# A four-stage decoder kernel: 32-wide heads moved to quarters of the array, score blocks issued in pairs, and the last stage's tail put in the order of one batch after the other

## The chip, the cores and the metric

The kernel runs on one core of a Trainium2 chip. The time is the device time of one execution in microseconds. Before the change it was 4651.4 us, the median of three runs (4647.05 to 4660.06).

## The reference

The input `x` is four batches of 512 tokens by 256 channels. It passes six sublayers, each with a residual and a layer norm. All matrix products are in 32-bit floats unless the text says otherwise.

```
x = LN(x + L0_attn(x))          # 16 heads of 64, with a zero key
x = LN(x + L0_xattn(x, ctx))    # 16 heads of 16, masked; softmax(q k^T / 4, -1e9 where mask == 0) v
x = LN(x + L0_ffn(x))           # top-2 of 8 experts
x = LN(x + L1_attn(x))          # 4 state-space layers with a scan over the 512 tokens
x = LN(x + L1_xattn(x, ctx))    # see below
x = LN(x + L1_ffn(x))           # gate, up and down with rounded activations and ternary weights

L1_xattn: x1 = LN(x + (x Wv) Wsa)                       # the self attention sees only its own token
          x2 = LN(x1 + MHA(x1, ctx) Wmha)               # 8 heads of 32, 512 keys
          y  = LN(x2 + relu(x2 W1) W2)
```

## The kernel before

Five engines run programs written out by hand and meet by counting semaphores: TensorE (`pe`, PE in the profile), VectorE (`v`, DVE), ScalarE (`act`, ACT), GpSimd (`pool`, POOL) and the queue of loads and stores (`sp`, SP). On each engine the instructions stand in program order. A wait holds back everything behind it on its engine. PSUM has eight banks of 512 words, `PS[:, 0..7, :]`.

The stages follow one another: for each of the four batches attention A (`AT_A`, 16 heads of 64) and attention B (`AT_B`, the masked one, its heads of 16 padded to 32), then the experts, then the state-space layers, then the last stage (`AT_E`, 8 heads of 32, and the feed-forward part), which takes the batches in two rounds `r` of a pair `p = 0, 1`.

**An attention** is `attend`, written once for each engine. A step `i` is two heads by 128 query tokens. B has 32 steps, E 16 for each batch. In the steady state a step goes through these hands:

- PE multiplies queries by keys into two of four score banks (L1147).
- DVE takes the row maxima. In B it adds the mask on the way and writes the sum to `b_S` in SBUF (L1589, then L1592 for the sign). In E one instruction does it (L1597).
- ACT takes the exponentials and their sums (L806).
- DVE inverts the sums (L1615), and POOL scales the probabilities (L641).
- PE transposes the probabilities of the step three before (L1159) into banks 4 and 5. DVE copies bank 4 (L1604) and ACT copies bank 5 (L816) to `pT`.
- PE multiplies the values by the transposed probabilities, one of four key blocks for each step (L1176), into bank 6 or 7.

In one turn of its loop PE does scores of step `i`, transposes of step `i - 3`, values of step `i - 7`. The next transposes wait for both copies of the last ones (`pt_a`, `pt_v`), since they go to the same banks.

A step of four-heads-to-128-rows attention (`per == 4`: B and E) takes two heads that lie in different halves of the array's rows. The queries are stored twice, each copy with every second strip of 32 rows zeroed, so that a product over 64 rows yields one head. ACT makes both copies (`pj_q`, L788). The value product writes 32 PSUM rows for each of the two heads, 512 columns each.

**The last stage** runs every phase for batch 0 of the pair and then for batch 1: context and its keys and values, layer norm 3, value and output projection, layer norm 4, queries, both attentions, output projection, layer norm 5, first and second linear layer of both batches, layer norms 6 and 7 of both, rounding of both, the loop of the feed-forward part over eight tiles (the batches alternate), layer norm 8 of both, and the stores. `sum_up` adds the residual to each tile and then, in one instruction, the bias (L1930). `ln_a` is the statistics and `ln_b` the rest of a layer norm.

Of the kernel before, what the change touches and what calls it, by code (L numbers as in the profile page):

```python
# [43 lines left out]
Q_WIDE = 2  # L44
# [9 lines left out]
class Count:  # L54
# [3 lines left out]
    def __init__(self, n, p, starts=None, batches=4):  # L58
        self.n, self.p, self.first = n, p, batches * p
        self.starts = tuple(starts or (p,)) + (n,)  # L60
# [4 lines left out]
    def two(self, b, u):  # L65
        k = max(i for i, at in enumerate(self.starts[:-1]) if at <= u)
        at, end = self.starts[k:k + 2]
        return self.first + b.r * 2 * (self.n - self.p) + 2 * (at - self.p) + b.p * (end - at) + (u - at)

    def __call__(self, b, u):  # L70
        return self.one(b, u) if u < self.p else self.two(b, u)


PJ = Count(PJ_N, PJ_EK, (PJ_EK, PJ_EV, PJ_EQ, PJ_L1))
TM = Count(TM_N, TM_EV, (TM_EV, TM_SA, TM_MHA, TM_L2))
TR = Count(TR_N, TR_CB, (TR_CB, TR_LND, TR_E1, TR_E2))
# [3 lines left out]
class LnCount:  # L80


    def __call__(self, b, i):
        return b * 2 + i if i < 2 else b + 8 if i == 2 else 12 + b.r * 12 + (i - 3) * 2 + b.p
# [41 lines left out]
def decoder(nc, d, out):  # L126
# [11 lines left out]
    with ExitStack() as ctx:  # L138
# [35 lines left out]
        strip01 = sb("strip01", [P, 2])  # L174
        qs_b = sb("qs_b", [P, 2])
        qs_e = sb("qs_e", [P, 2])
        qb_b = sb("qb_b", [P, 2, 4])
        qb_e = sb("qb_e", [P, 2, KC])
# [161 lines left out]
        ar = Arena(at_xt)  # L340
        f_h = ar([P, 4, F])
# [4 lines left out]
        f_hT = ar([P, 4, FC, P], BF16)  # L346
# [63 lines left out]
        def head(j, q, per):  # L410

            return 2 * j + q if per == 2 else 4 * (j // 2) + j % 2 + 2 * q
# [40 lines left out]
        def _(sp):  # L453
# [93 lines left out]
            def pair_loads(b):  # L547
                sp.dma_start(c_x(b), d["x2"][b.b].rearrange("(t p) n -> p t n", p=P)).then_inc(ld_x2[b.p], 16)
                sp.dma_start(ctx_b(b), d["ctx"][b.b].rearrange("(t p) n -> p t n", p=P)).then_inc(ld_cb[b.p], 16)

            c_out(0)
            for i in range(N_ITEM):
                l, b = i // B, i % B
                for n in range(N_STATE):
# [4 lines left out]
                    if n == 1 and i == N_ITEM - 1:  # L559
# [5 lines left out]
                        pair_loads(Two(0, 0))  # L565
# [10 lines left out]
            pair_loads(Two(0, 1))  # L576
# [6 lines left out]
            for p in range(2):  # L583
                sp.wait_ge(ln_mv, LN(Two(0, p), 7) + 1)
                pair_loads(Two(1, p))
# [176 lines left out]
        def _(act):  # L762
# [20 lines left out]
            def pj_q(b, u, qT, c, nc, scale, bias):  # L783


                act.wait_ge(pj_ps, PJ(b, u) + 1)
                for k in range(2):
                    ins = act.activation(qT[:, k * nc + c, :], PS[:, place(PJ, b, u, 4), :], ACT.Identity,  # L788
                                         bias=bias[:, k, c:c + 1], scale=scale[:, k:k + 1])
                ins.then_inc(pj_ev, 1)  # L790

# [4 lines left out]
            def attend(b, at, n, src, zero_key, probs, pT):  # L796
                s0, g0 = AT(b, at), GT(b, at // 4)
                for i in range(n + LAG):
                    if i < n:
                        s = s0 + i  # L800
                        act.wait_ge(smax, s + 1)
                        if i >= 4:
                            act.wait_ge(pt_ps, s - 3)
                            act.wait_ge(den_ok, s - 3)
                        for q in range(2):
                            ins = act.activation(probs[:, i % 4, q, :], src(i, q), ACT.Exp,  # L806
                                                 bias=nm[:, i % 4, q:q + 1], accum_out=sm[:, i % 4, q:q + 1])
                        if zero_key:
                            ins = act.activation(e0[:, i % 4, :], nm[:, i % 4, :], ACT.Exp)
# [1301 lines left out]
```

## Time and profile before

| | us |
|---|---|
| median of three runs | 4651.4 |
| profiled execution | 4649.78 |
| its span, first to last instruction | 4648.1 |
| one attention B, first scores to the end (four of them) | 117.5 |
| one attention E (four of them) | 57.0 |
| last stage | 715 |

The span is divided by the clock that the profiler kept, so every place below is given in microseconds from the start of the span. A busy share of an engine is a share of time in which a record of it is open, and matmul records overlap. The 1.7 us between the span and the execution's own time lie outside the records.

### The profile page before, as it was taken

The page shows a single profiled execution, that of the slowest core. Times are in us where ns is not written, and L with a number is a line of the kernel's source. Part 1 is how long each engine was busy: PE and PEld are TensorE (multiplying, and loading weights), DVE is VectorE, ACT ScalarE, POOL GpSimd, SP SyncE. Part 2 cuts the span into 40 slices and gives each one's busy share as a digit, 9 for nine tenths or more (in the row PEclk, how much of TensorE's full clock was granted, in tenths as well). Part 3 has the DMA queues.
Part 4 walks back from the last instruction along what each step waited for, and adds up shares of the span by engine and source line. Part 5 has one row for each costly group of instructions (what it writes and reads, how often), then busy time and mean ns, then how long its engine had stood idle before and what let it go on. Part 6 is the DMA issues. An engine that isn't in the chain of part 4 may idle for free. (4 is left out here: it accounts for less than half of the span.)

```text
span 4648.1 us, 46710 instructions
## 1 busy us (share of the span) xinstructions
PE 3953.6 (85%) x14986; PEld 2031.9 (44%) x14992; DVE 3108.6 (67%) x4273; ACT 2307.0 (50%) x4217; POOL 2283.4 (49%) x1206
## 2 busy tenths in 40 slices
PE   7888888888868997589999999999999987785785
PEld 3434434433438997233333333333333333434433
DVE  3464565455462111299999999999999998546546
ACT  3454444444442222476666666666666663432432
POOL 2353343344340001477877787878887785220220
PEclk9999999999989999799999999999999998898998
DMA  6000000000017886111111111111111120000000
GB/s 217 19 1 15 19 5 10 19 5 10 10 54 306 312 313 250 49 32 37 47 35 39 35 40 44 35 39 34 47 35 39 35 91 31 1 1 19 9 1 9
DMA packets 102377, 272.86 MB, mean 59 GB/s; under 512 B 9777, under 2 KB 55729, under 8 KB 96401
## 3 DMA queue, kind: packets, MB, share of 16 engines
q1 hardware_dynamic: 97216, 256.75, 16.1%
q0 software_dynamic: 4944, 13.51, 0.8%
q8 instruction: 102, 1.67, 0.1%
q14 instruction: 115, 0.93, 0.1%
HBM read 237.32 MB, written 32.90 MB: 58 GB/s over the span
## 5 line engine op out<-in xcount | busy, mean ns | idle before, releaser
L742 POOL TENSOR_TENSOR AR<-AR 128x1024 f32<-128x1024 f32 x512 | 1216.5, 2382 | 415.6 <-DVE AR L1852 339.1
L1852 DVE TENSOR_TENSOR_SCAN AR<-AR,PS 128x1024 f32<-128x1024 f32 x512 | 1170.6, 2286 | 17.6
L641 POOL TENSOR_TENSOR AR<-AR,rden 128x1024 f32<-128x1024 f32 x320 | 605.7, 1893 | 1121.7 <-DVE rden L1615 1055.5
L1385 PE MATMUL PS<-AR,ident 128*128 128x512 f32 x2048 | 1023.4, 627 | 32.2 <-POOL AR L742 31.7
L1005 ACT ACTIVATE AR<-AR,mcol 128x511 f32<-128x511 f32 x1024 | 668.0, 712 | 140.5 <-DVE AR L1852 138.1
L1846 DVE TENSOR_TENSOR PS<-AR,PS 128x1024 f32<-128x1024 f32 x512 | 628.1, 1227 | 78.6 <-PE PS L1370 59.6
L1385 PEld LDWEIGHTS PS<-AR,ident 128*128 128x128 f32 x2048 | 371.3, 194 | 479.2 <-issue 412.3
L1159 PE MATMUL PS<-ident,AR 128*128 128x128 f32 x2560 | 344.9, 278 | 122.1 <-issue 66.9
L1159 PEld LDWEIGHTS PS<-ident,AR 128*128 128x128 f32 x2560 | 276.5, 142 | 381.2 <-issue 360.5
L1147 PE MATMUL PS<-AR 64*128 64x512 f32 x1280 | 364.5, 650 | 50.9 <-ACT AR L806 24.0
L806 ACT ACTIVATE AR<-PS,nm 128x512 f32<-128x512 f32 x384 | 260.1, 683 | 295.4 <-DVE nm L1595 219.2
L1176 PE MATMUL PS<-AR 128*32 128x512 f32 (+1 forms) x1280 | 331.8, 608 | 0.0
L1272 PE MATMUL PS<-AR 128*128 128x128 f32 x2496 | 287.8, 277 | 8.1 <-ACT AR L863 8.1
L1299 PE MATMUL PS<-AR 128*128 128x512 f32 x512 | 259.8, 632 | 40.6 <-ACT AR L983 26.3
L1272 PEld LDWEIGHTS PS<-AR 128*128 128x128 f32 x2496 | 287.5, 194 | 10.5 <-ACT AR L863 8.5
L1123 PE MATMUL PS<-AR 128*128 128x512 f32 x608 | 282.0, 623 | 9.7 <-ACT AR L776 4.5
L1589 DVE CUSTOM_DVE_ANT_0 AR<-PS,AR 128x512 f32<-128x512 f32 x256 | 166.7, 689 | 166.0 <-PE PS L1147 131.2
L1131 PE MATMUL PS<-AR 128*128 128x256 f32 (+1 forms) x896 | 242.1, 432 | 38.6 <-DVE AR L1646 18.0
L1604 DVE COPY AR<-PS 128x512 f32<-128x512 f32 x320 | 220.2, 688 | 77.1 <-PE PS L1159 73.4
L806 ACT ACTIVATE AR<-AR,nm 128x512 f32<-128x512 f32 x256 | 182.6, 714 | 175.0 <-DVE nm L1592 174.8
L1328 PE MATMUL PS<-AR 128*128 128x512 f32 x512 | 240.6, 593 | 6.3 <-ACT AR L909 4.0
L1794 DVE TENSOR_TENSOR AR<-PS,AR 128x512 f32<-128x512 f32 x78 | 53.9, 692 | 271.9 <-ACT AR L872 271.9
(266 smaller groups left out, 4726.2 us busy)
## 6 DMA issues: line engine op xcount, KB each, us to landing
AR<-in_xw SPq DMA_DIRECT2D x39, 3072.0 KB, 10.5
AR<-mid_cs SPq DMA_DIRECT2D x256, 256.0 KB, 3.3
mid_xs<-AR SPq DMA_DIRECT2D x32, 512.0 KB, 7.9
AR<-mid_xs SPq DMA_DIRECT2D x39, 128.0 KB, 9.6
mid_ys<-AR POOLq DMA_DIRECT2D x39, 128.0 KB, 7.9
AR<-in_ctx SPq DMA_DIRECT2D x8, 512.0 KB, 5.0
AR<-in_mask SPq DMA_DIRECT2D x4, 1024.0 KB, 5.3
mid_x<-AR SPq DMA_DIRECT2D x8, 512.0 KB, 3.0
```

Source lines behind the costliest of these rows:

```text
L641: pool.tensor_tensor(probs[:, i % 4], probs[:, i % 4], rden[:, i % 4, :].rearrange("p (q o) -> p q o", o=1).to_broadcast([P, 2, 512]), ALU ...
L742: pool.tensor_tensor(m_HC[:, W % 3], m_H[:, W % 3, :].rearrange("p (c s) -> p c s", c=2), m_cb[:, n % 4:n % 4 + 1, :].to_broadcast([P, 2, ...
L806: ins = act.activation(probs[:, i % 4, q, :], src(i, q), ACT.Exp, bias=nm[:, i % 4, q:q + 1], accum_out=sm[:, i % 4, q:q + 1])
L1005: ins = act.activation(m_dA[:, W % 4, c, 1:512], m_dl[i % 2][:, cc, 1:512], ACT.Exp, scale=mcol[:, i // B, at:at + 1])
L1123: ins = pe.matmul(PS[:, place(PJ, b, u, 4), :], w[:, k, c * P:(c + 1) * P], xT[:, k, :], start=k == 0, stop=k == kc - 1)
L1147: ins = pe.matmul(PS[:, 2 * (i % 2) + q, :], qT[r:r + 64, part + h // per, t * P:(t + 1) * P], kT[r:r + 64, h // per, :], start=True, stop ...
L1159: ins = pe.transpose(PS[:, 4 + q, c * P:(c + 1) * P], probs[:, k % 4, q, c * P:(c + 1) * P], ident[:])
L1176: ins = pe.matmul(PS[p0:p0 + wide, 6 + bank % 2, :], V[:, c, h * wide:(h + 1) * wide], pT[j % 2][:, q, c, :], start=c == 0, stop=c == 3)
L1272: ins = pe.matmul(PS[:, bank, f * P:(f + 1) * P], w[:, kc, f0:f0 + P], x_T[:, kc, :], start=kc == 0, stop=kc == KC - 1)
L1385: ins = pe.matmul(PS[:, 2 * hf + c, :], ident[:], m_HC[:, W % 3, c, :], start=False, stop=n == NS - 1)
L1846: v.tensor_tensor(PS[:, 4:6, :], m_du[i % 2][:, 2 * hf:2 * hf + 2, :], PS[:, 6:7, :].to_broadcast([P, 2, 512]), ALU.mult).then_inc(d_bx, 1)
L1852: v.tensor_tensor_scan(m_H[:, W % 3, :], m_dA[:, W % 4].rearrange("p c s -> p (c s)"), PS[:, 4:6, :].rearrange("p c s -> p (c s)"), 0.0, A ...
```

## The change

It has four parts.

1. **Quarters.** Each head of 32 rows is multiplied in its own strip of 32 rows, over 32 rows, so the queries are stored once (`pj_q` is gone). A group of four steps now holds four heads by 256 query tokens, where it held two heads by 512. The values' product of one key block is four products of 256 columns in four strips of 32 columns of the array, where it was two products of 512 columns. `step_of` gives the new order of steps, `part_of` the place in `pT`. This holds for B and E.
2. **Score blocks in B.** In a turn PE does transposes and values first, and at every second turn the scores of two steps, which wait for the maxima of the step before (`smax`), not for its exponentials (`probs_ok`).
3. **B on DVE and ACT.** Both copy transposed probabilities before the maxima or exponentials of the turn, and DVE takes the reciprocals of odd steps ahead of the maxima of the next one.
4. **Last stage.** Biases are added before the sums they belong to are ready. The context work of the second round stands in the first round, between the two batches' linear layers. After the attentions the batches follow one another: layer norms 6 and 7 and the rounding of batch 0 stand beside the linear layers of batch 1, the feed-forward loop takes all four tiles of batch 0 first, and layer norm 8 of batch 0 stands in that loop. The context loads are issued apart from those of `x2`, and first.

```diff
 # tensor engine, attend
-                for i in range(n + LAG + 4):
+                def scored(i):
                     if i < n:
-                        s, t = s0 + i, i % T
-                        if i >= 2:
+                        s = s0 + i
+                        if not masked and i >= 2:
                             pe.wait_ge(probs_ok, s - 1)
-                        for q in range(2):
-                            h = head(i // T, q, per)
-                            r = 64 * q
-                            part = h % 2 * (qT.shape[1] // 2) if per == 4 else 0
...
+                        if masked and i % 2 == 0 and i >= 2:
+                            pe.wait_ge(smax, s)
+                        for e in ((i,) if not masked else (i, i + 1) if i % 2 == 0 else ()):
+                            j, t = step_of(e, per)
+                            for q in range(2):
+                                h = head(j, q, per)
+                                r = h % per * wide
+                                ins = pe.matmul(PS[:, 2 * (e % 2) + q, :], qT[r:r + wide, h // per, t * P:(t + 1) * P],
+                                                kT[r:r + wide, h // per, :], start=True, stop=True)
+                            ins.then_inc(scores, 1)
...
+                        for q in range(per):
+                            h = per * bank + q
+                            p0 = q * wide
+                            n0 = 0 if per == 2 else u % 2 * 256
...
+                            ins = pe.matmul(PS[p0:p0 + wide, 6 + bank % 2, n0:n0 + 1024 // per], V[:, c, h * wide:(h + 1) * wide],
+                                            moved[:, q, c, :], start=c == 0, stop=c == 3)
...
+                for i in range(n + LAG + 4):
+                    if not masked:
+                        scored(i)
+                        moved_on(i)
+                        summed(i)
+                    else:
+                        moved_on(i)
+                        summed(i)
+                        scored(i)
 # scalar engine, attend
                 for i in range(n + LAG):
+                    if i >= LAG and at == AT_B:
+                        copy(i - LAG)
                     if i < n:
...
+                        exps(i)
+                    if i >= LAG and at != AT_B:
+                        copy(i - LAG)
 # vector engine, attend
                 for i in range(n + LAG + 5):
                     s = s0 + i
+                    if masked:
+                        copy(i - LAG)
+                        if i % 2 == 0:
+                            inverse_of(i - 1)
 # scalar engine, queries of B (those of E alike)
                 for c in range(4):
-                    pj_q(b, PJ_BQ + c, b_qT, c, 4, qs_b, qb_b)
+                    pj(b, PJ_BQ + c, b_qT[:, c, :], ACT.Identity, 0.25, cols[:, C_BQ + c:C_BQ + c + 1])
 # vector engine, last stage
+                first, second = pair
+                sum_up(first, TM_L2)
+                ln_a(first, 6, e_R[0])
+                for b in ahead:
+                    context(b)
+                ln_b(first, 6, e_R[0], R_L3G, R_L3B)
...
+                for b in ahead:
+                    values_e(b)
+                ln_b(first, 7, e_X[0])
+                done(first, 7)
+                quantised(first)
+                quantised_T(first)
+                sum_up(second, TM_L2)
+                ln_a(second, 6, e_R[1])
+                hidden(pair, 0)
...
+                quantised(second)
+                hidden(pair, 1)
+                quantised_T(second)
+                for k in range(2, 8 + F_LAG):
+                    if k < 8:
+                        hidden(pair, k)
+                    down(pair, k - F_LAG)
+                    if k - F_LAG == T - 1:
+                        v.wait_ge(f_acc, r * 8 + T)
+                        ln_a(first, 8, e_X[0])
+                    if k - F_LAG == T:
+                        ln_b(first, 8, e_X[0])
```

What stands on TensorE in the steady part of attention B, two turns of the loop, before (L1147 scores, L1159 transposes, L1176 values; the register rows hold the semaphore counts of the loop over batches):

```order
L1142 REGISTER_ALU
L1147 MATMUL PS<-AR 128x512 x2
L1159 MATMUL PS<-ident,AR 128x128 x8
L1176 MATMUL PS<-AR 32x512 x2
L1142 REGISTER_ALU
L1147 MATMUL PS<-AR 128x512 x2
L1159 MATMUL PS<-ident,AR 128x128 x8
L1176 MATMUL PS<-AR 32x512 x2
```

The same two turns now (L1194 scores, L1207 transposes, L1229 values):

```order
L1188 REGISTER_ALU
L1194 MATMUL PS<-AR 128x512 x4
L1201 REGISTER_ALU
L1207 MATMUL PS<-ident,AR 128x128 x8
L1229 MATMUL PS<-AR 32x256 x4
L1207 MATMUL PS<-ident,AR 128x128 x8
L1229 MATMUL PS<-AR 32x256 x4
```

Two score blocks of two products have become one of four, and each value block has twice the products at half the width.

TensorE in the last stage from the output projection of the attention on, first round, before (L1131 products by tokens, L1116 and L1428 transposes, L1123 products by channels, L1440 gate and up, L1448 transposes of the hidden layer, L1455 down):

```order
L1131 MATMUL PS<-AR 128x256 x16
L1116 MATMUL PS<-ident,AR 128x128 x16
L1123 MATMUL PS<-AR 128x512 x32
L1131 MATMUL PS<-AR 128x256 x64
L1428 MATMUL PS<-ident,AR 128x128 x16
L1440 MATMUL PS<-wgu,AR 128x512 x24
L1448 MATMUL PS<-ident,AR 128x128 x8
L1455 MATMUL PS<-wdn,AR 128x256 x8
```

The same now (L1175, L1160, L1167 and L1487, L1500, L1509, L1518 in their places):

```order
L1175 MATMUL PS<-AR 128x256 x16
L1160 MATMUL PS<-ident,AR 128x128 x16
L1167 MATMUL PS<-AR 128x512 x16
L1175 MATMUL PS<-AR 128x256 x32
L1160 MATMUL PS<-ident,AR 128x128 x16
L1167 MATMUL PS<-AR 128x512 x8
L1175 MATMUL PS<-AR 128x256 x16
L1167 MATMUL PS<-AR 128x512 x16
L1487 MATMUL PS<-ident,AR 128x128 x8
L1175 MATMUL PS<-AR 128x256 x32
L1500 MATMUL PS<-wgu,AR 128x512 x16
L1487 MATMUL PS<-ident,AR 128x128 x8
```

The third to the seventh of these rows are batch 0's two linear layers and the context work of the next round. Batch 1's linear layers follow, with the transposes of batch 0's rounded input between them.

VectorE after batch 1's second linear layer, first round, before (L1928 residual sums, L1930 bias, L1897 and L1900 statistics, L1914 and L1918 the norm's two passes, L2025 the outer residual):

```order
L1928 TENSOR_TENSOR AR<-PS,AR 128x256 x4
L1930 TENSOR_TENSOR AR<-AR 128x1024
L1897 BN_STATS bst_e<-AR 128x6 x4
L1900 BN_AGGR mv_e<-bst_e 128x2 x4
L1907 RECIPROCAL rstd_e<-std_e 128x4
L1914 SCALAR_TENSOR_TENSOR AR<-AR,mv_e 128x256 x4
L1918 SCALAR_TENSOR_TENSOR AR<-AR,rstd_e 128x256 x4
L1907 RECIPROCAL rstd_e<-std_e 128x4
L1914 SCALAR_TENSOR_TENSOR AR<-AR,mv_e 128x256 x4
L1918 SCALAR_TENSOR_TENSOR AR<-AR,rstd_e 128x256 x4
L2025 TENSOR_TENSOR AR<-AR 128x1024
```

The same place now (L2013, L1982, L1985, L1992, L1999 in their places, L2045 to L2053 the hidden layer's tile 0 of batch 0):

```order
L2013 TENSOR_TENSOR AR<-PS,AR 128x256 x4
L1982 BN_STATS bst_e<-AR 128x6 x4
L1985 BN_AGGR mv_e<-bst_e 128x2 x4
L2045 SCALAR_TENSOR_TENSOR AR<-PS,fq,AR 128x512 x2
L2048 TENSOR_REDUCE fq<-AR 128x1
L2049 TENSOR_SCALAR fq<-fq 128x1
L2050 RECIPROCAL fq<-fq 128x1
L2051 TENSOR_SCALAR fq<-fq,wmean 128x1
L2052 TENSOR_SCALAR AR<-AR,fq 128x1024
L2053 TENSOR_SCALAR AR<-AR 128x1024
L1992 RECIPROCAL rstd_e<-std_e 128x4
L1999 SCALAR_TENSOR_TENSOR AR<-AR,mv_e 128x256 x4
```

Where both batches' norms stood behind one another, only batch 1's are left, and one hidden tile of batch 0 stands between its statistics and its passes. The bias sum is gone from this place.

## Rows read from the trace of the kernel before

**Rows 1.** The page: span and busy shares.

```profile
span 4648.1 us, 46710 instructions
PE 3953.6 (85%) x14986; PEld 2031.9 (44%) x14992; DVE 3108.6 (67%) x4273; ACT 2307.0 (50%) x4217; POOL 2283.4 (49%) x1206
```

**Rows 2.** Busy time by stretch: an attention B, an attention pair E, tails.

```profile
core 0: us, PE busy (x) PEld busy (x) DVE busy (x) ACT busy (x) POOL busy (x), PEclk, DMA share, GB/s
...
1242.00:1357.00 115.00, 96.61 (x504) 41.65 (x506) 72.54 (x227) 67.37 (x163) 60.57 (x32) 1.00 0.00 1
...
4018.00:4132.00 114.00, 98.16 (x512) 42.73 (x512) 64.56 (x100) 65.22 (x163) 60.56 (x32) 1.00 0.00 1
```

**Rows 3.** Timeline of attention B, one pair of steps (start, us, engine, line).

```profile
600.86 1.13 PE L1147 MATMUL PS<-AR 64*128 64x512 f32 x4
...
602.23 0.69 DVE L1589 CUSTOM_DVE_ANT_0 AR<-PS,AR 128x512 f32<-128x512 f32 x1 [1.48 <-PE PS L1147]
...
603.78 0.72 ACT L806 ACTIVATE AR<-AR,nm 128x512 f32<-128x512 f32 x1 [1.84 <-DVE nm L1592]
...
605.20 0.57 ACT L816 ACTIVATE AR<-PS 128x512 f32<-128x512 f32 x1
...
605.88 1.06 PE L1159 MATMUL PS<-ident,AR 128*128 128x128 f32 x8 [0.73 <-issue]
...
606.87 1.05 PE L1176 MATMUL PS<-AR 128*32 128x512 f32 x4
...
607.86 1.13 PE L1147 MATMUL PS<-AR 64*128 64x512 f32 x4
```

**Rows 4.** Timeline of attention E, one pair of steps.

```profile
4383.19 1.13 PE L1147 MATMUL PS<-AR 64*128 64x512 f32 x4
...
4384.37 1.23 DVE L1597 TENSOR_REDUCE nm<-PS 128x2 f32<-128x1024 f32 x1 [1.29 <-PE PS L1147]
...
4385.63 0.69 ACT L806 ACTIVATE AR<-PS,nm 128x512 f32<-128x512 f32 x1 [1.65 <-DVE nm L1597]
...
4388.66 1.05 PE L1176 MATMUL PS<-AR 128*32 128x512 f32 x4
...
4389.64 1.13 PE L1147 MATMUL PS<-AR 64*128 64x512 f32 x4
```

**Rows 5.** The chain that ended last: values at an attention's end, transposes at 1.2 GHz.

```profile
4324.78 6.87 PE PS L1123 x16
...
4352.30 1.94 PE PS L1116 x8
...
4472.23 4.51 PE PS L1176 x20
```

**Rows 6.** Busy time by stretch around a fall of TensorE's clock.

```profile
409.90:413.30 3.40, 1.72 (x8) 0.60 (x8) 2.25 (x5) 2.75 (x10) 1.59 (x1) 1.00 0.00 0
...
413.30:416.70 3.40, 3.40 (x14) 2.08 (x12) 3.06 (x7) 2.06 (x6) 2.19 (x2) 0.50 0.00 0
```

**Rows 7.** Groups by line: ScalarE's two copies of the queries; VectorE's bias sums.

```profile
L788 ACT ACTIVATE AR<-PS,qb_b,qs_b 128x512 f32<-128x512 f32 x32 | 23.1, 773 | 12.5 <-PE PS L1123 12.5
...
L1930 DVE TENSOR_TENSOR AR<-AR 128x1024 f32<-128x1024 f32 x12 | 14.7, 1225 | 0.4
```

**Rows 8.** Busy time by stretch: linear layers, norms, round two's context, feed-forward loop, end.

```profile
4157.00:4214.30 57.30, 57.27 (x193) 37.00 (x192) 6.59 (x17) 11.89 (x18) 0.00 (x0) 0.96 0.00 1
...
4293.40:4324.60 31.20, 22.16 (x80) 15.52 (x81) 20.44 (x65) 5.39 (x11) 0.00 (x0) 0.77 0.10 34
...
4559.10:4582.50 23.40, 0.00 (x0) 0.00 (x0) 22.69 (x67) 2.17 (x4) 0.00 (x0) 0.60 0.00 0
4582.50:4593.50 11.00, 6.15 (x22) 4.13 (x24) 6.04 (x14) 0.69 (x1) 0.00 (x0) 0.50 0.00 0
4593.50:4638.10 44.60, 30.32 (x185) 18.37 (x185) 38.79 (x72) 20.28 (x32) 0.00 (x0) 0.96 0.00 1
```

**Rows 9.** The page's loads and stores: the output (line, KB each, us to landing).

```profile
out<-AR SPq DMA_DIRECT2D x4, 512.0 KB, 3.0
```

More of the change, by code:

```diff
@@ L76, with in_pairs @@
-TR = Count(TR_N, TR_CB, (TR_CB, TR_LND, TR_E1, TR_E2))
+        return self.one(b, u) if u < self.p else self.at[b.r, b.p, u]
+def in_pairs(ahead, both, apart):
+    order = [(0, q, g) for g in ahead for q in range(2)]
+    for r in range(2):
+        order += [(r, q, g) for g in both for q in range(2)]
+        order += [(r, 0, g) for g in apart]
+        if r == 0:
+            order += [(1, q, g) for g in ahead for q in range(2)]
+        order += [(r, 1, g) for g in apart]
+    return order
@@ new lines, in down @@
+            def down(pair, k):
+                n = pair[0].r * 8 + k
+                pe.wait_ge(f_hq, n + 1)
+                for c in range(FC):
+                    ins = pe.transpose(PS[:, 4 + c // 4, (c % 4) * P:(c % 4 + 1) * P],
+                                       f_h[:, n % 4, c * P:(c + 1) * P], ident[:])
+                ins.then_inc(f_ht, 1)
+                pe.wait_ge(f_hta, n + 1)
+                if k == 0:
+                    pe.wait_ge(f_xv, pair[1].b + 1)
+                if k >= 2:
+                    pe.wait_ge(f_acc, n - 1)
+                for c in range(FC):
+                    ins = pe.matmul(PS[:, 6 + n % 2, 0:D], f_hT[:, n % 4, c, :], wdn[:, c, :],
+                                    start=c == 0, stop=c == FC - 1)
+                ins.then_inc(f_o, 1)
@@ L1466, in _, with context @@
+            def context(pair):
+                for b in pair:
+                    pe.wait_ge(ld_cb[b.p], (b.r + 1) * 16)
                     tr(b, TR_CB, ctx_b(b))
@@ L1982, in _ @@
                 pair = (Two(r, 0), Two(r, 1))
-                for b in pair:
-                    tr_ev(b, TR_CB, e_CT[b.p][:, 1, :])
+                ahead = (Two(r + 1, 0), Two(r + 1, 1)) if r + 1 < B // 2 else ()
+                if r == 0:
+                    for b in pair:
+                        context(b)
                 for b in pair:
@@ L2000, in _ @@
                 for b in pair:
[L2001 removed]
+                    with_bias(b, R_SAB, e_X[b.p])
+                for b in pair:
+                    sum_up(b, TM_SA)
                     ln_a(b, 4, e_R[b.p])
@@ new lines, in _ @@
+                done(first, 6)
+                own.link(v.tensor_tensor(e_X[0], e_X[0], e_R[0], ALU.add))
+                ln_a(first, 7, e_X[0])
+                for b in ahead:
+                    values_e(b)
+                ln_b(first, 7, e_X[0])
[4 more added lines that the diff above has]
+                ln_a(second, 6, e_R[1])
+                hidden(pair, 0)
+                ln_b(second, 6, e_R[1], R_L3G, R_L3B)
@@ new lines, in _ @@
+                done(second, 6)
+                own.link(v.tensor_tensor(e_X[1], e_X[1], e_R[1], ALU.add))
+                ln_a(second, 7, e_X[1])
+                ln_b(second, 7, e_X[1])
+                done(second, 7)
+                quantised(second)
+                hidden(pair, 1)
+                quantised_T(second)
+                for k in range(2, 8 + F_LAG):
+                    if k < 8:
+                        hidden(pair, k)
+                    down(pair, k - F_LAG)
+                    if k - F_LAG == T - 1:
+                        v.wait_ge(f_acc, r * 8 + T)
+                        ln_a(first, 8, e_X[0])
+                    if k - F_LAG == T:
+                        ln_b(first, 8, e_X[0])
```

480 lines of the change are left out of this document (235 added, 245 removed).

## The prediction

> **What bounds the kernel now.** I read the page first. TensorE has the largest busy share, 85% [rows 1], but that is an average over stages, and the change touches only three kinds of them: four attentions B, four attentions E, and the rest of the last stage. So I read busy time by stretch. In an attention B no engine is full: in 115 us TensorE's records cover 96.6, VectorE's 72.5, ScalarE's 67.4, GpSimd's 60.6, and the clock is granted in full [rows 2]. An attention pair E looks the same [rows 2]. Records of matmuls overlap and outlast the streaming, so 97 of 115 is not a full engine.
>
> What holds the steps is a loop through three engines, and the timeline of one pair of steps shows it [rows 3]. Scores start at 600.86. The maxima start at 602.23 (1.37 later), the exponentials at 603.78 (1.55), ScalarE's copy of older transposes at 605.20 (1.42, it stands behind both exponentials), the next transposes, which need that copy, at 605.88 (0.68), the values at 606.87 (0.99), and the scores two steps on at 607.86 (0.99). The sum is 7.00 us for two steps. E has the same loop [rows 4]: 1.18 to the maxima, 1.26 to the exponentials, 3.03 to the values, 0.98 to the next scores, 6.45 for two steps. TensorE's order and these waits fix the pace; each of its blocks behind the copy counts in full.
>
> In the last stage it changes hands. Over the linear layers TensorE's records cover 57.3 of 57.3 us; then it has nothing for 23.4 us, in which VectorE works 22.7 on the norms and the rounding; 11.0 us go to the move into the feed-forward loop, and in the loop's 44.6 us VectorE has 38.8 [rows 8].
>
> **The value product, both attentions.** A product of 32-bit floats leaves two records. Sixteen records of 512 columns take 6.87 us in a row, 0.43 each [rows 5], while four of a value or score block take about 1 us from block to block [rows 3]: two strips run side by side, two records deep, 2 x 0.43, and 0.12 around them. Four strips side by side of 256 columns would be 2 x 0.215 and 0.12, thus 0.55 for 0.98: 0.43 less. The block lies on the loop once for each pair. B: 15 pairs beyond the start give 6.5 us, and four value blocks stand alone at the end (five took 4.51 [rows 5]) and give 1.7: 8.2 us each, 33 for four. E: seven pairs and some two blocks at the end, 4 us each, 16 for four.
>
> The bounds: if four strips are no faster than two, nothing; if they are, this. I take the whole, since two strips already run without loss.
>
> **Scores in B.** A block of four quarters replaces two blocks of two halves, 1.13 us for 2.26 if the quarters run side by side. This I cost at nothing on the loop: it still goes from a score block over one step's maxima, both exponentials, the copy, one set of transposes and one value block to the next score block, 1.37 + 1.55 + 1.42 + 0.68 + 0.99 + 0.55 = 6.56. ScalarE's copy now stands ahead of the exponentials of its turn, but behind those of the turn before, which are late ones; the first copy is early, the second is not. The same with VectorE's copy and the reciprocals: GpSimd waits for them and takes 60.6 of 115 us [rows 2], it is not on the loop. What covers the second score block's absence is idle time of TensorE: its blocks sum to 1.13 + 2 x 1.02 + 2 x 0.55 = 4.27 of 6.56, where they were 6.2 of 7.00. Thus 2.3 us idle in one piece, waiting for the copy, where it was 0.73 [rows 3].
>
> **TensorE's clock.** That idle piece has a price. Before, the clock stood at 2.4 GHz through the attentions [rows 2]. But at an attention's start a stretch of 3.4 us with 1.72 us of records at 2.4 GHz was followed by one at 1.2 GHz [rows 6]. The new loop has such stretches around each idle piece. At 1.2 GHz eight transposes take 1.94 us [rows 5] for 1.06 [rows 3], 0.88 more; scores stream 0.86 longer and values 0.43, so 2.2 us on a pair whose blocks all meet it. Ends: 0, and 2.2 for all 64 pairs, 140 us. Before it rose again TensorE's records covered 3.40 of 3.40 us in that row, as a slower loop would make them here; I take two pairs of each sixteen, 18 us in all, nearer the lower end as the clock has recovered after one stretch in the nearest row. E's blocks still cover 5.4 of 6.0, so nothing there.
>
> **Queries.** ScalarE copied each query chunk twice at 773 ns [rows 7], and the scores wait for the last. One copy takes away 0.8 us before the first scores, four times in B, twice in E: 5 us.
>
> **Bias sums.** Each took 1.2 us [rows 7]. After the value and the attention projections two stand on VectorE's path to the layer norm, in each round: 10 us. Put ahead, they meet VectorE idle while TensorE projects, so they cost nothing there; without that cover they would cost the same 10.
>
> **The tail, second round.** Before, from the end of the linear layers to the last sum: 23.4 + 11.0 + 44.6 = 79.0 [rows 8], and 6.5 more to the end of the last norm (the span's last 10.0 us [rows 1] less the store's 3.0 [rows 9] and its issue). Now the linear layers end 2.2 later (1.0 for the transposes of batch 0's rounded input, 1 for a wait of the second layer on the first's last copy). Behind them stand on VectorE: batch 1's sum and statistics 2.2; a wait of 2.5 while ScalarE turns from the square root to the activation of tile 0; tile 0, 4.6; batch 1's two norms and rounding, half of 22.7 with a little wait, 12.2; tile 1 and two copies 5.8; six tiles at 38.8 / 8 = 4.85, 29; norm 8 of batch 0 with a turn of ScalarE's function, 5.8; the last two down products 4.8; batch 1's norm 3.7. Sum 70.6. So 2.2 + 70.6 for 85.5: 12.7 less. The first norm behind batch 1's linear layers is hidden (half of 57.3 us of TensorE's work [rows 8] beside some 16 of VectorE's); if it weren't, 10 of these 12.7 would be gone.
>
> **First tail and second head.** The same 12.7 less, but the context work, 16 transposes, four chunks and eight tiles, some 18 us of TensorE (2 + 7 + 7 at 0.43 for a record of 512 columns, and a wait for VectorE), now stands in the tail, and batch 0's norm 8 counts there too: the last sum comes 8 later than before. The head behind it took 31.2 us [rows 8] and now holds only norm 8 of batch 1, the outer sum, norm 3 and its transposes, and the store of batch 1's output, which must land (3.0 us [rows 9]) before its buffer is written: 15 to 17. Net 7.5 less. The new order of loads (context first) saves under 1.
>
> **The sum** against the profiled execution's 4649.8: 33 + 16 + 5 + 10 + 12.7 + 7.5 = 84, less 18 for the clock, 66: 4584. The median of the runs lies 1.6 above that execution, so 4585.
>
> A rule speaks against the quarters. The Trainium skill, "TensorE: Matmul & The Clock Gate", section "Measured speedup vs the span model", gives 3.07 times for four row strips where side by side would be 4. The trace's pairs show no such loss, and no row shows four. By the rule a score or value block streams 1.3 times as long, an estimate of 29 us more in all.
>
> **Rivals.**
> - *The clock doesn't fall in B.* For it: transposes and values are dense around the piece. Against: rows 6. 4650 + 1.6 - 84 = 4567. Chance 0.2.
> - *Four strips share something that two don't.* If a block streams a third longer: 0.86 becomes 1.14 once for each B pair (18 us), 0.43 becomes 0.57 on 64 B and 32 E pairs (13), so 4585 + 30 = 4615. For it: four moving operands where the trace has two. Against: two run with no loss. 0.13.
> - *The gain of B is eaten by the clock, or the last stage's order gives nothing.* The waits of ScalarE between its functions are my least sure terms. 20 us either way: 4605. 0.14.
> - *Slower: TensorE runs B at 1.2 GHz.* The loop's pair becomes 6.56 + 2.2 = 8.8 for 7.0; 140 us over my loop, 4585 - 18 + 140 = 4707. It turns the sign once the pairs lose 84 us, when three pairs in five are wholly at 1.2 GHz. Against: the clock has come back after one dense stretch. 0.06. Strips of 32 rows running in turn would do it too (3.7 us for a block of 1.13); 0.02.
> - *It doesn't do what it says:* the score blocks' order changes no time, which is in the forecast already.
>
> My forecast has 0.45. **Range:** 4556 (the clock holds, and the tails give ten more) to 4615 (the third rival's or the second's time) holds 0.8. About 0.3%, 14 us, is what these runs can tell from no change. Faster 0.89, the same 0.04, slower 0.07.
>
> **What the profile would show.** Value blocks in B and E 0.55 apart from the next block, not 0.98; score blocks in B of eight records in 1.13. Pairs of steps of 6.6 in B with ScalarE's copy as what TensorE's transposes wait for, and 6.0 in E. Granted clock in an attention B 0.85 to 0.95, not 1.00. No stretch of 23 us without TensorE in the last stage; second head under 20 us. The prediction is wrong if value blocks stay at 0.98, if B's clock is near 0.5, or if the last stage's tail has new waits on ScalarE above 5 us.

## The result, and the profile after

The changed kernel took 4624.4 us (median of 4 runs, 4616.9 to 4628.1) against 4651.6 us for the kernel before on the same chip (4 runs, 4647.1 to 4660.1): a ratio of 0.9937, 95% interval 0.9918 to 0.9956. It is faster by 27 us, where 66 were forecast, and 4624.4 lies 9 us above the range.

The page of the changed kernel, to be read beside [rows 1]: span and busy shares, then the granted clock of TensorE in 40 slices.

```profile
span 4623.7 us, 48219 instructions
PE 3874.9 (84%) x15752; PEld 2047.3 (44%) x15760; DVE 3104.6 (67%) x4259; ACT 2299.0 (50%) x4201; POOL 2283.0 (49%) x1206
...
PEclk9989999999989998799999999999999999788788
```

TensorE's records shrank by 79 us and the span by 24. The last six slices hold the attentions E and the feed-forward work; 7 and 8 there say that the clock was low for a part of them.

The busy time by stretch (columns as in [rows 2]): two attentions B, the first pair of attentions E whole, then the first 27.3 us of its first attention, and the rest of that one.

```profile
core 0: us, PE busy (x) PEld busy (x) DVE busy (x) ACT busy (x) POOL busy (x), PEclk, DMA share, GB/s
1230.00:1345.00 115.00, 75.69 (x637) 41.91 (x640) 71.13 (x227) 67.17 (x162) 60.54 (x32) 0.93 0.00 1
563.50:678.50 115.00, 76.84 (x648) 42.75 (x649) 72.95 (x229) 66.95 (x162) 60.42 (x32) 0.93 0.00 1
3997.90:4122.30 124.40, 107.52 (x640) 54.01 (x640) 65.39 (x100) 64.78 (x163) 60.57 (x32) 0.78 0.00 1
4002.30:4029.60 27.30, 27.30 (x94) 13.34 (x92) 13.22 (x20) 14.01 (x38) 14.04 (x8) 0.50 0.00 0
4029.60:4060.00 30.40, 25.23 (x220) 13.06 (x216) 16.61 (x27) 15.32 (x38) 16.15 (x9) 1.00 0.00 1
```

In [rows 2] the clock was 1.00 in both. Now it is 0.93 in B (in the second of these rows five falls of 3.4 us each; 0.90 in the first attention B), and in E it falls 4.4 us after the first scores and stays at 0.50, 1.2 GHz, for 27.3 us, in which TensorE's records cover 27.30. The same happens in each attention E (27.3, 27.3, 23.9, 27.3 us). A pair E takes 124.4 and 122.6 us, where it took 114.1 both times. So the smaller share of TensorE in the whole hides an attention E that is slower than before.

The timeline of one pair of steps in an attention B (start, duration, engine, line; it answers to [rows 3]). L1194 is the score product, L1207 the transposes, L1229 the values, L1687 VectorE's maxima, L827 the exponentials, L837 ScalarE's copy.

```profile
601.97 1.14 PE L1194 MATMUL PS<-AR 32*128 32x512 f32 x8
...
603.04 1.09 PE L1207 MATMUL PS<-ident,AR 128*128 128x128 f32 x8
...
603.33 0.69 DVE L1687 CUSTOM_DVE_ANT_0 AR<-PS,AR 128x512 f32<-128x512 f32 x1 [1.06 <-PE PS L1194]
...
604.88 0.72 ACT L827 ACTIVATE AR<-AR,nm 128x512 f32<-128x512 f32 x1 [2.55 <-DVE nm L1690]
...
606.31 0.57 ACT L837 ACTIVATE AR<-PS 128x512 f32<-128x512 f32 x1
...
606.98 1.06 PE L1207 MATMUL PS<-ident,AR 128*128 128x128 f32 x8 [2.27 <-ACT AR L837]
...
607.97 0.64 PE L1229 MATMUL PS<-AR 128*32 128x256 f32 x8
...
608.54 1.14 PE L1194 MATMUL PS<-AR 32*128 32x512 f32 x8
```

From scores to scores: 1.36, 1.55, 1.43, 0.67, 0.99 and 0.57, together 6.57 us for 7.00 before. Eight quarter scores take 1.14 us (the transposes behind them start after 1.07), and eight value records of 256 columns hold their place for 0.57: here four strips side by side lose nothing against two. The copy is what the transposes wait for, and TensorE is idle 2.27 us ahead of them. Where the clock was low a pair took 7.89 in the steady part of the attention, and up to 8.8 at the start of the first one.

The chain of work that ended last, at the start of an attention E (start, duration, piece):

```profile
4011.20 2.01 PE PS L1194 x4
4013.21 1.90 PE PS L1207 x8
4015.11 2.01 PE PS L1194 x4
4017.11 1.90 PE PS L1207 x8
4019.01 2.01 PE PS L1194 x4
```

Each piece begins where the one ahead ends: at 1.2 GHz TensorE alone sets the pace, 3.91 us a step. At 2.4 GHz, later in the same attention, it is 6.04 us for two steps, as forecast. TensorE's rows of the timeline:

```profile
4041.29 1.13 PE L1194 MATMUL PS<-AR 32*128 32x512 f32 x4
4042.38 1.07 PE L1207 MATMUL PS<-ident,AR 128*128 128x128 f32 x8
4043.37 0.64 PE L1229 MATMUL PS<-AR 128*32 128x256 f32 x8
4043.94 1.13 PE L1194 MATMUL PS<-AR 32*128 32x512 f32 x4
4045.76 1.07 PE L1207 MATMUL PS<-ident,AR 128*128 128x128 f32 x8 [0.69 <-issue]
4046.76 0.64 PE L1229 MATMUL PS<-AR 128*32 128x256 f32 x8
4047.33 1.13 PE L1194 MATMUL PS<-AR 32*128 32x512 f32 x4
```

The last stage by stretch (it answers to [rows 8]): round one's linear layers with round two's context work among them, the head of round two, round two's linear layers, the longest stretch without TensorE behind them, and the feed-forward loop.

```profile
4142.40:4221.00 78.60, 75.66 (x266) 49.56 (x266) 25.43 (x63) 15.90 (x25) 0.00 (x0) 0.96 0.02 7
4288.60:4299.60 11.00, 0.04 (x1) 0.00 (x0) 10.24 (x35) 1.13 (x4) 0.00 (x0) 0.68 0.13 48
4483.20:4547.95 64.75, 60.48 (x202) 38.65 (x202) 20.87 (x53) 11.74 (x19) 0.00 (x0) 0.94 0.00 1
4557.10:4569.86 12.76, 0.08 (x1) 0.00 (x0) 12.01 (x35) 2.85 (x4) 0.00 (x0) 0.50 0.00 0
4569.86:4613.70 43.84, 30.76 (x173) 20.31 (x176) 38.47 (x79) 18.49 (x29) 0.00 (x0) 0.85 0.04 13
```

The 23.4 us without TensorE are now 12.8, since the norms of the first batch lie beside the second's linear layers (VectorE 20.87 us there, 6.59 before). But those layers take 64.7 us for 57.3, and the timeline shows a hole of 3.49 us in them:

```profile
4523.00 0.38 DVE L1985 BATCH_NORM_AGGREGATE mv_e<-bst_e 128x2 f32<-128x6 f32 x4
4523.41 0.30 ACT L1069 ACTIVATE std_e<-mv_e,epsc 128x4 f32<-128x4 f32 x1 [6.78 <-DVE mv_e L1985]
4523.62 2.40 ACT L812 ACTIVATE AR<-PS,cols 128x512 f32<-128x512 f32 x4
...
4524.34 8.83 PE L1167 MATMUL PS<-AR 128*128 128x512 f32 x16 [3.49 <-ACT AR L812]
```

ScalarE stands 6.78 us at the square root of batch 0's layer norm 7, for VectorE's statistics. Batch 1's copies out of the first linear layer (L812) are queued behind it, and TensorE waits for the first of them.

### The profile page after: what moved, and what is told of

The parts are those of the page before. It is cut to its first block, busy times and chain, and to the rows that moved or that the text cites. A ratio compares the mean times of both kernels' runs of the same rounds, so it can differ in the third digit from the quotient of the medians.

```text
span 4623.7 us, 48219 instructions
## 1 busy us (share of the span) xinstructions
PE 3874.9 (84%) x15752; PEld 2047.3 (44%) x15760; DVE 3104.6 (67%) x4259; ACT 2299.0 (50%) x4201; POOL 2283.0 (49%) x1206
## 4 chain that ended last, share of the span: by engine, by line
PE 36%; issue 18%; DVE 18%; POOL 18%; ACT 9%; SPq 1%; DMA 0%; POOLq 0%; DVEq 0%; ACTq 0%
POOL AR L672 11%; DVE AR L1937 7%; PE PS L1448 7%; PE PS L1335 6%; DVE PS L1931 4%; PE PS L1391 4%; POOL AR L773 3%; PE PS L1345 3%; PE PS L1362 3%; PE PS L1167 3%; ACT AR L1033 2%; PE PS L1175 2%; PE PS L1194 2%; PE PS L1207 2%; PE PS L1441 1%
## 5 line engine op out<-in xcount | busy, mean ns | idle before, releaser
L1448 PE MATMUL PS<-AR,ident 128*128 128x512 f32 x2048 | 1021.3, 626 | 33.5 <-POOL AR L773 33.3
L1448 PEld LDWEIGHTS PS<-AR,ident 128*128 128x128 f32 x2048 | 370.4, 193 | 479.5 <-issue 412.6
L1207 PE MATMUL PS<-ident,AR 128*128 128x128 f32 x2560 | 384.7, 299 | 202.5 <-ACT AR L837 159.3
L1207 PEld LDWEIGHTS PS<-ident,AR 128*128 128x128 f32 x2560 | 307.8, 153 | 453.2 <-issue 388.7
L827 ACT ACTIVATE AR<-PS,nm 128x512 f32<-128x512 f32 x384 | 260.0, 682 | 317.2 <-DVE nm L1693 218.8
L1194 PE MATMUL PS<-AR 32*128 32x512 f32 (+1 forms) x1280 | 321.2, 719 | 47.5 <-DVE nm L1690 13.3
L1167 PE MATMUL PS<-AR 128*128 128x512 f32 x608 | 286.5, 630 | 13.2 <-ACT AR L807 4.5
L827 ACT ACTIVATE AR<-AR,nm 128x512 f32<-128x512 f32 x256 | 182.7, 715 | 171.2 <-DVE nm L1690 170.1
L1229 PE MATMUL PS<-AR 128*32 128x256 f32 (+1 forms) x2048 | 260.6, 462 | 2.3 <-DVE AR L1658 1.2
L1175 PE MATMUL PS<-AR 128*128 128x256 f32 (+1 forms) x896 | 235.2, 422 | 32.5 <-DVE AR L1731 18.0
L1687 DVE CUSTOM_DVE_ANT_0 AR<-PS,AR 128x512 f32<-128x512 f32 x256 | 166.1, 686 | 100.5 <-PE PS L1194 99.9
```

Of the source, the lines that this page charges most:

```text
L1167: ins = pe.matmul(PS[:, place(PJ, b, u, 4), :], w[:, k, c * P:(c + 1) * P], xT[:, k, :], start=k == 0, stop=k == kc - 1)
L1194: ins = pe.matmul(PS[:, 2 * (e % 2) + q, :], qT[r:r + wide, h // per, t * P:(t + 1) * P], kT[r:r + wide, h // per, :], start=True, stop=True)
L1207: ins = pe.transpose(PS[:, 4 + q, c * P:(c + 1) * P], probs[:, k % 4, q, c * P:(c + 1) * P], ident[:])
L1448: ins = pe.matmul(PS[:, 2 * hf + c, :], ident[:], m_HC[:, W % 3, c, :], start=False, stop=n == NS - 1)
```

## The experiments

Two theories of the attentions. **Strips:** score products over 32 rows let the granted clock fall, whatever stands around them. **Idle or short values:** the clock falls because the loop has more idle time, or because the value products have 256 columns. Each row of busy time below is of one stretch, with the columns of the stretches above. "Low" is time at the granted clock 0.50. Only the changed kernel and experiments 7 and 9 have four runs; the others have one, and runs of one kernel differ by up to 13 us (the kernel before took 4645.3 to 4658.1 in 7 runs beside experiments 5 to 8), so what single runs are asked lies in their stretches. Experiments 1 to 4 ran on one chip (the kernel before: 4648.7 there), 5 to 8 on another (4648.4), 9 and 10 on a third (4646.1), and the changed kernel beside a before of 4651.6. So totals are best compared by what each took off the kernel before beside it; the change took off 27.

**1. E wholly as before,** B and the last stage changed. The edit in words:

```diff
-    h = 2 * j + q;  r = h % 4 * 32;  rows r .. r+32 of q and k
+    h = 4 * (j // 2) + j % 2 + 2 * q;  r = 64 * q;  rows r .. r+64, queries doubled with zeros (pj_q)
-    values: four heads, 256 columns each
+    values: two heads, 512 columns each
```

> The changed kernel with attention E wholly as before (scores over halves of the rows with the doubled queries, values in two products of 512 columns); B and the last stage's order stay changed. Both theories expect the clock in E back at 2.4 GHz and each attention E at 57.0 us (62.4 in the changed kernel), so about 4 x 5 = 20 us less, 4603, less some 1.6 us for the second copy of the queries: 4605. If instead the new order of the last stage had slowed the attentions, they would stay above 60.

It took 4610.2 us, 38 off its before. The first pair E:

```profile
4000.30:4115.20 114.90, 99.59 (x512) 43.27 (x512) 65.27 (x100) 64.78 (x163) 60.56 (x32) 0.99 0.00 1
```

The clock is back (low for 3.4 and 6.8 us in the two pairs), and the two pairs E take 231.2 us for the 247.0 of the changed kernel.

**2. E with scores over 64 rows and values in quarters.** As 1, with the value products of the change kept.

> Attention E with scores over halves (64 rows) but values in quarters (four products of 256 columns). Theory strips (products over 32-row strips are what lowers the clock, since only half of the rows are then at work): clock at 2.4 GHz, pairs of steps 6.0 us, each attention E 53.3, total about 4590. Theory short values (the value blocks' shorter streaming leaves TensorE too idle, whatever the strips): clock falls in E as in the changed kernel, each attention near 62, total about 4625.

4588.7 us, 60 off its before, 33 more than the change took off.

```profile
3993.60:4100.50 106.90, 85.61 (x640) 43.28 (x640) 65.93 (x100) 64.62 (x162) 60.56 (x32) 1.00 0.00 1
```

The clock is 1.00, with TensorE covered for 85.6 of 106.9 us, less than in any other E: more idle time and short value products don't lower it. In this kernel's timeline two steps take 6.02 us, the same as quarters at full clock.

**3. The opposite mix in E:** scores over 32 rows, values of two heads and 512 columns.

> The other half: attention E with scores over 32-row quarters, values as before in two products of 512 columns. Theory strips: the clock falls in E, each attention above 60 us, total 4625 to 4640. Theory short values: clock 2.4 GHz, each attention 57.0, total about 4604.

4627.4 us, pairs of 129.2 and 128.9, low 23.9 us in each attention.

```profile
3990.50:4119.70 129.20, 119.31 (x512) 52.95 (x512) 65.33 (x100) 65.08 (x163) 60.56 (x32) 0.82 0.00 1
```

TensorE is covered for 92% of the stretch and the clock is low all the same. With the changed kernel the three make a full table of the first pair E: scores over 64 rows take 114.9 us with values of two heads (1) and 106.9 with values in quarters (2), scores over 32 rows 129.2 (3) and 124.4 (the change). With either kind of values it is the rows of the scores that bring the long low clock, 48 and 55 us of it in that pair (3 and the change) for 3.4 and 0 (1 and 2). So the strips theory holds in E, and the rival has fallen. What no run separates is the 32 rows of a product from the 64 of 128 rows that are at work in a block of two such products, since in E every block of quarters has both.

**4. B in the order of before,** quarters kept: score blocks ahead of the transposes, one step at a time, copies behind the exponentials, every reciprocal behind the maxima.

```diff
-attend(b, AT_B, 32, b_qT, b_kT, b_V, 4, OT_B, True, probs, pT)
+attend(b, AT_B, 32, b_qT, b_kT, b_V, 4, OT_B, False, probs, pT)
```

> The changed kernel with attention B's quarters kept but its order undone: one score block of two quarters in every turn ahead of the transposes, waiting for the exponentials two steps before; copies and reciprocals behind the maxima. The loop's sum is the same 6.56 us for two steps at 2.4 GHz. Theory strips: blocks of two quarters bring the clock down in B for long stretches, as in E of the changed kernel, B's attentions 120 us or more, total 4650 or above. Theory short values: TensorE has more to do than in the changed kernel (5.4 of 6.6 us), the clock holds, B's attentions near 109.5, total about 4610.

4627.9 us, 22 less than strips was to give; B takes 117.6, 117.6, 117.6 and 118.1, below the 120 of that theory and well above the rival's 109.5. It is low for 27 us in one piece at the start in the first three, as in E, and for 31 in the last, 23.8 of it in one piece. The second of them:

```profile
562.60:680.20 117.60, 97.30 (x640) 48.02 (x640) 73.00 (x228) 66.92 (x163) 60.57 (x32) 0.88 0.00 1
```

The order of the change breaks that piece up (17 to 24 us low, lengths 117.7, 114.1, 114.1, 116.2 in the changed kernel). But five traces hold this same code of B, those of the changed kernel and of experiments 1, 2, 3 and 10, and in them a B takes 115.2 to 117.1 us on average. So, against the 117.7 of one trace, the order is worth 0.6 to 2.5 us for each B, as a remedy for the quarters.

**5. and 6. Scores over 64 rows and values in quarters in B and in E,** with B in the order of before (5) and in that of the change (6).

> Attentions B and E both with scores over halves and values in quarters, and B in its order of before. Theory strips: the clock stays at 2.4 GHz in B too (17 to 24 us of 105 at 1.2 GHz in the changed kernel), pairs of steps 6.57 us throughout, each B 109.5 us for 113.8 to 117.6 in e_halves_quadval; total 4588.7 - 4 x 6.5 + 3 (second copies of the queries) = 4565. Rival: B is throttled because its loop leaves TensorE idle, whatever the strips; then B stays near 116 and the total near 4590.

> The same with B's changed order (score blocks of two steps behind the transposes, reciprocals of odd steps first). The loop's sum is the same, 6.57 us a pair, and with halves the pair of score blocks takes 2.26 us again, so this adds up to the same as halves_quadval_old if the order is worth nothing: 4565, within 3. If the order matters by itself (idle pieces of TensorE in one place, the first steps), it shows as falls of the clock or as longer starts: 4570 to 4585.

4585.1 and 4587.6 us. The second attention B of 5, then of 6:

```profile
559.40:670.60 111.20, 87.46 (x640) 43.52 (x640) 73.03 (x228) 66.93 (x162) 60.64 (x32) 0.98 0.00 1
```

```profile
560.50:672.80 112.30, 85.33 (x640) 45.07 (x640) 74.18 (x228) 66.87 (x162) 59.98 (x32) 0.97 0.00 1
```

B's are 111.7, 111.2, 111.8, 110.8 in 5 and 112.3 (112.1 the last) in 6; low 0 to 3.5 us in 5, and 6.8 (3.5 in the last) in 6. With the clock kept, the order of the change gains nothing, 0.9 us lost for each B.

The totals missed their expectations, by 20 us in 5 and by 23 in 6. For 5 the traces show where. Its B's are 19 us shorter together than those of experiment 2, where 26 were expected (111.4 on average for 109.5): 7. Some 6 us more lie around the B's, where 3 were expected for the second query copies: 3. And from the last B's end to the first E scores 2 took 2646 us and 5 took 2655: 9. Most of that stretch, up to the last product of the state-space layers, no edit touches, and in the twelve traces it takes 2578 to 2587 us; the difference arises between 450 and 690 us into it. It goes with the chip that the kernel ran on: 2578 to 2581 in experiments 1 to 4, 2583 to 2587 in 5 to 8, 2578 and 2580 in 10 and 9, 2586 and 2585 in the traces of before and of the change. Why it varies is open; no run asked it.

**7. Experiment 5 with ScalarE's square root later:** in round two it stands behind four of the eight copies of batch 1.

```diff
+                early = 0 if ahead else 4
+                first_linear(pair[1], 0, early)
                 ln_e(pair[0], 7)
-                first_linear(pair[1])
+                first_linear(pair[1], early, FC)
```

> As halves_quadval_old, with ScalarE's square root of layer norm 7 of batch 0, in the second round, moved behind four of the eight chunks of batch 1's first linear layer instead of ahead of all eight. In the changed kernel TensorE waited 3.5 us and lost 1.8 more there at the clock's lower level: 5 us less than halves_quadval_old, 4560. If VectorE's path is what bounds the stretch, nothing is gained.

4577.9 us (4 runs, 4576.1 to 4586.6), 0.9849 of before, interval 0.9829 to 0.9869: the fastest kernel here, 70 off its before where the change took off 27. The 4560 expected rested on the 4565 of experiment 5, which had not come. The move itself did what it was to do: round two's linear layers take 60.9 us for the 64.3 of experiment 5. An attention B and the first pair E:

```profile
556.60:667.90 111.30, 87.42 (x640) 43.52 (x640) 73.06 (x228) 66.88 (x162) 60.58 (x32) 0.98 0.00 1
3986.80:4093.70 106.90, 85.60 (x640) 43.25 (x640) 65.86 (x100) 64.72 (x163) 60.56 (x32) 1.00 0.00 1
```

**8. The last stage's new order alone,** all attentions as before.

> The kernel before with only the last stage's new order (biases ahead, context work of round two in round one, batches one after another). By the phases of the changed kernel's trace outside its attentions (last stage 3.7 us shorter in spite of 18.7 us lost in the attentions E) and the earlier loads, it should give 22 to 26 us: 4625. My forecast had 35 for these terms (10 biases, 12.7, 7.5, and its queries).

4619.6 us against 4648.4 on that chip: 29 less. The pairs E themselves take 114.9 and 116.3 us (114.1 before), 3 more with 3.4 and 6.8 us of low clock where none was, so the gain is in what lies around them: by the traces 4.6 us in round one's head, 13.3 between the pairs and 11.1 behind the second.

**9. The value products in quarters alone,** in B and E, in the kernel before.

```diff
-    for q in range(2):
-        h = head(j, q, per);  p0 = h % per * wide
-        matmul(PS[p0:p0 + wide, 6 + bank % 2, :], V[..h..], pT[j % 2][:, q, c, :])
+    for q in range(4):
+        h = 4 * bank + q;  n0 = j % 2 * 256
+        matmul(PS[32 * q:32 * q + 32, 6 + bank % 2, n0:n0 + 256], V[..h..], quad_of(pT, 4 * j, q)[:, c, :])
```

> The kernel before with one part of the change alone: in B and E the value products of four heads side by side, 256 columns each (with the order of heads and tiles that this needs). Scores stay products over 64 rows with doubled queries, the order of all else stays as before. Value product worth what the prediction put down (0.43 us for each pair of steps): B 117.5 less 6.5 to 8.2 each, about 110 to 111, E 57.1 less 3.6 to 4, about 53.3, together 41 to 49 us less: 4602 to 4608. The clock should hold at 2.4 GHz nearly throughout both, if it is the score products over 32 rows that lower it. Rival: the drop of the clock comes from the shorter loop with more idle time of TensorE, or from value products in quarters; then B and E have 20 us and more at 1.2 GHz each and the time is 4640 or above.

4597.8 us (4 runs, 4595.0 to 4606.5), 0.9898 of before, interval 0.9881 to 0.9914: this part alone gains more than the whole change. The last B and the first pair E:

```profile
1222.50:1333.30 110.80, 85.90 (x640) 42.65 (x640) 73.51 (x228) 67.01 (x163) 60.64 (x32) 1.00 0.00 1
3985.30:4092.20 106.90, 85.58 (x640) 43.23 (x640) 65.94 (x100) 64.76 (x163) 60.64 (x32) 1.00 0.00 1
```

B's take 111.8, 111.3, 111.8 and 110.8 (117.5 to 118.5 before), the pairs E 106.9 and 108.1. That is 26 and 13 us. The rest of the 48 lies outside the attentions, 6.6 of it in the untouched stretch described under experiment 5. So the value products account for 39.

**10. The changed kernel with experiment 7's move alone.**

> The changed kernel with one move: in the second round ScalarE's square root for layer norm 7 of batch 0 stands behind four of the eight copies of batch 1's first linear layer, not ahead of them all. If the square root there stalled TensorE 3.5 us, in a trace of the changed kernel, at 4520.8, the wait goes, the second round's linear layers take 60 to 62 us for 64.7, and the whole is 3 to 5 less: 4620. Rival: the norm of batch 0 then ends later and VectorE, which bounds the tail, gives the same time back at the last down product: 4624, with the stretch behind the linear layers 3 to 4 longer.

4621.8 us, one run, 24 off its before (4646.1): its total can't tell it from the changed kernel, but its trace can. Round two's linear layers, from their first product to their last:

```profile
4483.37:4544.16 60.79, 58.49 (x201) 37.88 (x202) 20.87 (x53) 11.96 (x19) 0.00 (x0) 0.97 0.00 1
```

60.8 us for 64.7, and from their end to the span's end 75.9 for 75.8: the hole of 3.5 us is gone, with the 1.8 us that the low clock cost behind it, and nothing is given back behind. A smaller hole of 1.5 us stands in its place, ahead of the transposes of batch 0's rounded input, which the later norm delays: the rival's mechanism, in small. The gain of 3.9 us is what the expectation said.

## Why the prediction was wrong

The step that failed is "E's blocks still cover 5.4 of 6.0, so nothing there". It priced the clock by how much of the time TensorE is covered, and took from [rows 6] that a fully covered stretch brings the clock back. In E the records cover 27.30 of 27.30 us and the clock stays low. Experiments 1, 2 and 3 beside the changed kernel show that it hangs on the score products over 32 rows, whichever way the values are split. Against the same attention with scores over 64 rows (experiment 9: 106.9 and 108.1), the two pairs E lose 32 us, where 0 were put down. That alone carries 4585 to 4617. The rival in which TensorE runs at 1.2 GHz had B as its place and the idle piece as its cause; the place that decided was E.

The other steps, by the traces:

- **Value product, B 33 and E 16.** Experiment 9 gives 26 and 13. The loop's 0.43 for each pair was right (6.57 forecast 6.56; E 6.04 forecast 6.0), and so was the end of an attention: its last five value blocks took 4.53 us before and 2.82 in experiment 9, 1.7 less.

```profile
676.83 4.53 PE L1176 MATMUL PS<-AR 128*32 128x512 f32 x20
```

```profile
666.00 0.64 PE L1193 MATMUL PS<-AR 128*32 128x256 f32 x8
666.89 1.93 PE L1193 MATMUL PS<-AR 128*32 128x256 f32 x32 [0.26 <-ACT AR L831]
```

  What was wrong is the count of 15 pairs. The first value block stands seven steps behind the first scores, so the first pairs hold none. Score block by score block the two traces run alike for the first three pairs and then part by 0.41 us a pair: 12 pairs, 4.9 us from the first to the last scores of a B. In E four pairs hold it, where seven were counted. Mis-sized by 10.
- **The clock in B, 18.** B's of the change sum to 462.1 us, those of experiment 9 to 445.7: 16 lost (15 to 22 over the five traces with the same code of B). The size was right (granted clock 0.90 to 0.93, forecast 0.85 to 0.95), the reason was not: in experiment 4 the same quarters, with the idle piece shortened to 1.2 us by the order of before, are low for longer, and in 6 the order of the change over 64 rows is low for 6.8 us at most. The strips make most of it (462.1 for 449.0 in the same order), the order the rest (449.0 for 445.5 over 64 rows).
- **Four strips sharing something:** no. Eight quarter scores in 1.14, eight value records in 0.57. By the Trainium skill ("TensorE: Matmul & The Clock Gate", section "Measured speedup vs the span model") four row strips are measured at 3.07 times. The trace agrees with the figure: eight records at 0.43 us each would be 3.4 us in a row, and the block takes 1.14, 3.0 times less. What it does not bear out is the 1.3 times longer streaming that the prediction read into it, since two strips took 1.13 for four [rows 3] and so fell short of their factor in the same way.
- **Queries, 5.** From the first scores of A to those of B the four batches together take 2.6 us less (forecast 3.3); E's share doesn't stand apart.
- **Last stage, 10 + 12.7 + 7.5 = 30.** Experiment 8 gives 29. Inside the changed kernel terms were off against each other. Round two's linear layers take 7.4 longer, not 2.2: the hole of 3.5 us and 1.8 at the low clock behind it. The tail behind them gave 13.3 of a forecast 14.9. So the second round's tail is worth 5.9, not 12.7. Against it, each projection behind an attention E ends 4.1 earlier and round one's head, with loads and queries, is 4.3 shorter, 12.5 in all for the 10 of the bias sums. Round one's tail and the head behind it gave together 8.3 for 7.5 (10.9 and 18.6 less, 21.2 more in the linear layers with the context work).

The sum of what is found: E 32, value product 10, less 2 for the clock in B: 40 us, for a miss of 39. That it comes out so closely is in part luck, since the untouched stretch alone differs by 9 us between traces.

Of what the profile was to show: value blocks 0.57 apart, score blocks of eight in 1.14, pairs of 6.57 with the copy as what the transposes wait for, no stretch of 23 us without TensorE and a second head under 20 (15.9 us, 11.0 of it without TensorE) are all there. Of the granted clocks, the signs that the prediction would be wrong named B's alone; E's was not on the list.

## What to carry to other kernels

Splitting the output side in four (value products of 32 columns each into strips of 128 partitions, 256 columns moved) and splitting the contraction in four (scores over 32 rows) look alike in the count of records, but here only the first paid: 0.43 us off each pair, clock untouched. The second gained nothing on the loop that the waits set, 6.04 us for 6.02 with zero-padded 64 rows, and cost 8 us for each attention E in clock, with all the low clock in the attention's first 32 us. So price a change of the array's shape for the granted clock by a stretch in which TensorE does that shape, not by how much of the time it is covered, and move two such edits apart before joining them.

When an engine's queue takes on work of two batches, ask at each instruction that waits whose copies stand behind it: one square root cost TensorE 3.5 us and 1.8 more at the low clock, and putting four copies ahead of it gave 3.9 back.

## What the runs showed of the hardware that was not expected

- With TensorE's records covering all of a stretch (27.30 of 27.30 us) the granted clock stayed at 1.2 GHz, in attentions whose scores are products over 32 rows. With products over 64 rows padded with zeros, at the same 6.0 us for two steps, it was 1.00 over a pair. It rose again within the attention, 6.8 us after the first value block had joined the loop (4022.85 to 4029.6). The same holds in every attention where the clock was low in one long piece from its start, the sixteen E with quarter scores (the changed kernel, experiments 3, 4 and 10) and the four B of experiment 4: until the value products join TensorE does only such scores and transposes, and 1.8 to 6.9 us after they join the clock is back; in E it then stays at 1.00 to the attention's end. No run moved the value products, so that they bring it back is not shown.
- The same stretch of untouched work, from the last B to the end of the state-space layers, takes 2578 to 2587 us in kernels that differ elsewhere, and runs on one chip lie closer together (2578 to 2581 in four traces, 2583 to 2587 in four others).
